# Cross-attention and routed feed-forward: three quarters of the second layer in parts, its relus left in PSUM, and a low part in three pieces

## The reference, cut to what matters

```python
assign = jnp.argmax(x @ centroids.T, axis=1)          # one expert for each token
xn  = layernorm(x) * ln_g[e] + ln_b[e]
h   = relu(einsum('etd,efd->etf', xn, w1) + b1)        # 256 -> 1024
y   = x + einsum('etf,edf->etd', h, w2) + b2           # 1024 -> 256
out = a * y + (1 - a) * x,   a = sigmoid(x @ centroids.T)   # of the chosen expert
```

## Time and profile before

| | |
|---|---|
| median of 3 runs | 1052.74 us (1052.73 to 1053.05) |
| profiled execution, its own time | 1052.73 us |
| its span, first to last instruction | 1050.9 us |
| busy: PE / DVE / ACT / POOL | 1041.6 / 844.9 / 688.7 / 565.3 us |
| granted TensorE clock, mean | 0.999 of full speed |

### The profile page before, as it was taken

One profiled execution on the slowest core, in us unless ns is written; L12 is line 12 of the kernel. 1 busy time (PEld: TensorE's weight loads), 2 busy tenths in 40 slices (PEclk: granted clock), 3 DMA queues, 4 the chain that ended last, 5 costly groups with the idle time before them and its releaser, 6 DMA issues.

```text
span 1050.9 us, 24670 instructions
## 1 busy us (share of the span) xinstructions
PE 1041.6 (99%) x8610; PEld 940.5 (89%) x8610; DVE 844.9 (80%) x1979; ACT 688.7 (66%) x1838; POOL 565.3 (54%) x665
## 2 busy tenths in 40 slices
PE   9999999999999999999999999999999999999997
PEld 7889898988888888889898989889888999999997
DVE  7878888878888888888888879888887797767663
ACT  6765757675666767666757575766566666676761
POOL 1744464646454555545464646465444667566663
PEclk9999999999999999999999999999999999999999
DMA  6665657585757576767667585856356868777760
GB/s 212 160 169 148 170 156 189 146 215 142 201 146 197 142 193 155 200 156 197 159 168 185 142 210 137 213 144 171 91 153 196 307 198 294 250 234 234 249 194 31
DMA packets 159666, 190.57 MB, mean 181 GB/s; under 512 B 17454, under 2 KB 149038, under 8 KB 154673
## 3 DMA queue, kind: packets, MB, share of 16 engines
q1 hardware_dynamic: 155088, 179.09, 62.4%
q0 software_dynamic: 3360, 8.53, 2.2%
q10 hardware_dynamic: 1088, 1.31, 0.4%
HBM read 65.72 MB, written 46.07 MB: 106 GB/s over the span
## 4 chain that ended last, share of the span: by engine, by line
PE 96%; DVE 2%; POOL 1%; ACT 1%; DMA 0%; issue 0%; POOLq 0%; DVEq 0%
PE psum L742 17%; PE psum L775 16%; PE psum L812 11%; PE psum L902 10%; PE psum L791 10%; PE psum L827 9%; PE psum L761 8%; PE psum L938 6%; PE psum L932 5%; PE psum L830 1%; PE psum L883 1%; PE psum L914 1%; DVE neg_max L1410 1%; DMA c_in<-in_ctx_in 0%; PE psum L856 0%; DVE w_lo L1545 0%
## 5 line engine op out<-in xcount | busy, mean ns | idle before, releaser
L1823 POOL TENSOR_TENSOR prob<-prob,inv_sum 128x512 f32<-128x512 f32 x172 | 177.7, 1047 | 190.1 <-DVE inv_sum L1416 189.2
L1133 ACT ACTIVATE prob<-psum,neg_max 128x256 f32<-128x256 f32 x344 | 160.2, 478 | 38.8 <-DVE neg_max L1410 38.5
L1410 DVE TENSOR_REDUCE neg_max<-psum 128x2 f32<-128x512 f32 x256 | 161.9, 672 | 27.7 <-PE psum L791 27.5
L1422 DVE STREAM_TRANSPOSE prob<-prob 128x512 f32<-128x512 f32 x172 | 118.5, 698 | 12.3 <-POOL prob L1823 11.9
L1823 POOL TENSOR_TENSOR w_ring<-w_ring,inv_sum 128x512 f32<-128x512 f32 x76 | 78.1, 1041 | 76.0 <-DVE inv_sum L1416 75.7
L1140 ACT ACTIVATE head_out_hi<-psum 128x512 fp32r<-128x512 f32 x52 | 31.1, 597 | 105.6 <-PE psum L812 102.4
L1119 ACT ACTIVATE v_n<-psum 128x512 f32<-128x512 f32 x128 | 77.9, 608 | 26.7 <-PE psum L775 22.7
L1108 ACT ACTIVATE k_hi<-psum 128x512 fp32r<-128x512 f32 x128 | 77.0, 603 | 22.0 <-PE psum L742 21.3
L1461 DVE TENSOR_TENSOR k_lo<-psum,k_hi 128x512 fp32r<-128x512 f32 x128 | 85.7, 674 | 0.0
L742 PE MATMUL psum<-kv_t_hi,w_hi 128*128 128x512 f32 x252 | 85.0, 419 | 0.0
L775 PE MATMUL psum<-w_hi,kv_t_hi 128*128 128x512 f32 x256 | 80.2, 395 | 0.4 <-DVE k_lo L1461 0.4
(11 more groups left out here) (215 smaller groups left out, 2952.4 us busy)
## 6 DMA issues: line engine op xcount, KB each, us to landing
sorted_rows<-filler SPq DMA_DIRECT2D x54, 660.0 KB
prob_t<-prob SPq DMA_DIRECT2D x172, 128.0 KB, 2.8
w_ring<-prob SPq DMA_DIRECT2D x172, 128.0 KB, 2.7
w<-in_experts SPq DMA_DIRECT2D x19, 1024.0 KB, 7.8
w_ring<-in_experts SPq DMA_DIRECT2D x18, 1024.0 KB, 6.7
prob_t<-w_ring SPq DMA_DIRECT2D x76, 128.0 KB, 2.8
w_ring<-w_ring SPq DMA_DIRECT2D x76, 128.0 KB, 2.7
w_ring<-normed SPq DMA_DIRECT2D x56, 128.0 KB, 3.0
```

What stands on the lines that cost most here:

```text
L1133: act.activation(prob_at(u, bb)[:, :, parity, i], scores_i, ACT.Exp, bias=neg_max[:, at, i:i + 1], accum_out=prob_sum[:, at, i:i + 1]).the ...
L1410: dve.tensor_reduce(neg_max[:, (4 * u + n) % 8, :], psum[:, n, :].rearrange("p (i j) -> p i j", i=2), AXIS_X, ALU.max, negate=True).then_i ...
L1422: dve.transpose(probs, probs).then_inc(s_quad, 1)
L1823: pool.tensor_tensor(probs, probs, inverse, ALU.mult).then_inc(s_soft, 1)
```

## The change

FS goes from 4 to 6: six of the eight chunks of the second layer are in parts, two are plain. The relus of the chunks in parts are written back to the PSUM bank in which they lie, and VectorE splits from there. The bank is then free for the next slot's `layer_1` when VectorE has split it (`f_hl`), not when ScalarE has read it (`f_ha`). ScalarE no longer waits for `hid_raw` to be free, since there is none. GpSimd's low part of w2, now 1536 columns, is made in three instructions of 512; ScalarE's high part is one instruction of 1536. The buffers hid_hi and hid_lo grow and the spacer between them shrinks.

```diff
-            FS = FC // 2
+            FS = 3 * FC // 4
-                sbuf(late, "hid_between", [P, 3 * FS * BLOCK])
+                sbuf(late, "hid_between", [P, (2 * FC + FC // 2 - 2 * FS) * BLOCK])
-            hid_raw = y_t[:].rearrange("p c b t -> p c (b t)")
-            hid_plain = prob_t_even[:].rearrange("p b a h i s q -> p b (a h i s q)").rearrange("p s (f t) -> p s f t", f=FC - FS)
+            hid_plain = prob_t_even[:].rearrange("p b a h i s q -> p (b a h i s q)")[:, FC * BLOCK - 2 * (FC - FS) * BLOCK:].rearrange(
+                "p (s f t) -> p s f t", s=2, f=FC - FS)
 def layer_1(s):
                         if s == 1:
                             pe.wait_ge(s_exp, 8 * n_steps)
+                        elif i < FS // 2:
+                            pe.wait_ge(f_hl, FS // 2 * (s - 1 - FIRST_SPLIT) + i + 1)
                         else:
                             pe.wait_ge(f_ha, FC // 2 * (s - 2) + i + 1)
 def relu_parts(s):
                     if s == FIRST_SPLIT:
-                        wait_low(act, n_pairs - 1, 1)
                         wait_made(act, ("pv", n_steps - 1))
                     for i in range(FC // 2):
                         act.wait_ge(f_h, FC // 2 * (s - 1) + i + 1)
-                        if i < FS // 2 and s > FIRST_SPLIT:
-                            act.wait_ge(f_hl, FS // 2 * (s - 1 - FIRST_SPLIT) + i + 1)
-                        elif i == FS // 2 and s >= 2:
+                        if i == FS // 2 and s >= 2:
                             wait_made(act, ("fy", s - 2, 1))
-                            dst = hid_raw[:, i, at] if f < FS else hid_plain[:, s % 2, f - FS, :]
+                            dst = psum[:, i, at] if f < FS else hid_plain[:, s % 2, f - FS, :]
 def split_hidden(s):
-                        then_next(dve.tensor_copy(hi, hid_raw[:, i, :]))
-                        dve.tensor_tensor(lo, hid_raw[:, i, :], hi, ALU.subtract).then_inc(f_hl, 1)
+                        raw = psum[:, i, :]
+                        then_next(dve.tensor_copy(hi, raw))
+                        dve.tensor_tensor(lo, raw, hi, ALU.subtract).then_inc(f_hl, 1)
 def low_weights_2(s):
-                    pool.tensor_tensor(w2_hl[s % 2][1], raw, w2_hl[s % 2][0], ALU.subtract).then_inc(f_w2l, 1)
+                    hi, lo = w2_hl[s % 2]
+                    for f in range(0, FS, 2):
+                        last = pool.tensor_tensor(lo[:, f:f + 2], raw[:, f:f + 2], hi[:, f:f + 2], ALU.subtract)
+                    last.then_inc(f_w2l, 1)
```

## The result

| | before | after |
|---|---|---|
| median | 1053.05 us (1052.73 to 1054.95, 5 runs) | 1059.09 us (1058.34 to 1060.24, 5 runs) |
| profiled execution, its span | 1052.73, 1050.9 | 1058.34, 1056.5 |
| granted TensorE clock, mean | 0.999 | 0.996 |

The gain on TensorE is there; what it waits for costs twice as much. The busy line of the page after (us, share of the span, instructions), beside the earlier trace rows: TensorE's busy time fell by only 1.4 us, where 5.25 were taken out. That is the first sign that something in it grew.

A forecast was written before the change was run, and what follows sets the result against it. TensorE, busy 99% of the span, was taken as the bound, with VectorE nearly so around slots 1 to 5. 1052.7 - 5.25 (TensorE's work) + 4.2 (waits) = 1051.7 us; range 1049.5 to 1053.5, widened to 1049.0 and 1054.2 towards rivals.

The forecast's parts named there:

- TensorE, -5.25: TensorE's matmuls, 18 slots: two more chunks in parts save 0.29 us a slot, 5.25 us in all; slot 11.80 for 12.09.
- VectorE, the copy from PSUM at 0.67: VectorE's split of hidden banks: copying 512 columns from PSUM takes 0.67 us, so a bank takes 1.34 us.
- What that does to slots 1 to 5, +4.2: Early slots: VectorE's 6.7 us more work makes slot 5's input ready at 872.8; TensorE loses 4.2 us, earlier waits included.
- It does not come on top of the 4.2: Slot 1's late low part: TensorE would wait up to 1.7 us, but VectorE is then ahead by the same stretch.
- GpSimd in three pieces: GpSimd's low part of w2: three pieces of 512 columns take 3.1 to 3.6 us; VectorE's holds total taken as unchanged.
- holds VectorE for at most one piece at a time: GpSimd's low part: VectorE is held for at most one piece of some 1.2 us at a time, but over a longer stretch.
- the sum of the holds as unchanged: VectorE's holds under GpSimd's low parts: some 6 us before, 2.4 less to 1.2 more after; taken as unchanged.
- What costs nothing: ScalarE's longer high part, relus into PSUM (0 to 0.1 us), banks freed by VectorE, dropped waits, late slots' 1.5 us on VectorE.
- The rival on the other side: Late slots: VectorE becomes the bound, held for two pieces, slot 12.3 us, 6 us over 12 slots: 1057.7 us; chance 0.16.

The follow-up runs named there:

- the early low part: Changed kernel, but GpSimd makes the low part of slot 1's w2 before the row scales of the last batch: 1060.49 us, ratio 1.0071.
- the gap: Changed kernel, but GpSimd waits for its own piece of w2's low part to end before issuing the next: 1057.60 us, ratio 1.0043.
- one piece: Changed kernel with GpSimd's low part of w2 in one instruction of 1536 columns instead of three of 512: 1063.05 us, ratio 1.0097.
- the fill: Changed kernel with unused matmuls on TensorE ahead of its waits, four in slot 1's layer 2, eight at slot 5's layer_1: 1058.49 us, ratio 1.0046.
- the kernel from slot 5 on with GpSimd's wait: Changed kernel with four chunks in slots 1 to 4; GpSimd adds the base of slots 4 to 15 after VectorE's input split: 1058.59 us, ratio 1.0039.
- The input first: Changed kernel, but for slots 3 to 5 VectorE splits the next input after the first hidden bank, not the third: 1057.25 us, ratio 1.0039.

## Why the prediction was wrong, point by point

- *TensorE, -5.25:* right; 11.80 us a slot, layer_1 to layer_1.
- *VectorE, the copy from PSUM at 0.67:* right. All 54 casts of line 1644 take 676 to 693 ns and all 54 subtractions of line 1645 take 691 to 694, so none of them was ever held, where before line 1645 took 0.834 in the mean of the late slots. A bank's pitch is 1.32 us against 1.34.
- *What that does to slots 1 to 5, +4.2:* the place was right, and VectorE is what layer_1 waits for, but the input of slot 5 was ready at 876.69 and not at 872.8.
- *"It does not come on top of the 4.2":* this is the step that failed. TensorE's wait for slot 1's low part came (1.77 us; "up to 1.7" was its price), and VectorE's lead was to pay for it. VectorE could not keep the lead, since it needs that layer 2 itself: it stood idle for 0.59 + 2.07 = 2.66 us where the prediction had it without idle time. That is most of the 3.9 us by which slot 5's input was late; a start 0.5 us later, 0.4 us more of holds and 0.3 of the rest make up the others. This is read from the trace; the low part of slot 1 made early took that wait away, and the kernel was no faster, since a cast was then held for 4.60 us.
- *GpSimd in three pieces, "holds VectorE for at most one piece at a time", "the sum of the holds as unchanged":* the sum was right (7.5 us against 7.1 before), the first half was wrong. The cast of line 1628 was held for 3.40 us, through three pieces; with a wait of GpSimd between them no such cast or subtraction lasts over 1.80. That hold fell on the very instruction that TensorE was about to need: with the cast and the subtraction at 0.45 + 0.69 us the input would have been ready at 873.7, 0.4 us behind TensorE's asking at 873.32, and not 3.4. But shorter holds, tried by themselves, did not make the kernel measurably faster, since there were more of them and VectorE was late all the same (0.17 + 2.96 us of waits at layer_1). The Trainium skill, "SBUF — State Buffer", section "Who interferes with whom", says that a VectorE copy in a 2-port mode and GpSimd block each other for the whole instruction. The trace agrees that a copy within SBUF is held (0.42 us by itself, 3.40 here), but by that rule alone the hold would have ended with the piece that it met, at some 873.3 us.
- *The price of a wait:* a term that was missing. Waits of 1.77 and 3.46 us were each followed by matmuls at the lower clock, 1.7 us more apiece. The 1.73 behind slot 5 come on top of all the rest; those of slot 1 are part of why VectorE stood idle.
- *What costs nothing:* the last slot wasn't looked at (0.49 + 0.24 us); and GpSimd's pause near 905 us, 4.62 us long in the trace of before, was in view and not weighed. In the profiled execution of the change it happens to cost nothing, and nothing in two of the others with six chunks there (the early low part, the gap); in seven TensorE waited 1.4 to 4.7 us behind it, and in the last two (one piece, the fill) a wait of 2.77 and of 0.65 us stands a slot later, which wasn't followed up. It lasts 3.87 to 8.00 us, and not longer the later GpSimd comes to it: 3.87 from 906.95 on in the change, 7.74 from 902.65 on in the kernel from slot 5 on with GpSimd's wait. Why is open: the profile names no releaser.

In the prediction's own sum: TensorE's last matmul ends 6.3 us later than -5.25 and +4.2 have it. Slot 5's layer_1 begins 3.9 us late (876.79 for 872.85), the lower clock behind it takes 1.7 and the last slot 0.7. This is one profiled execution taken apart; how the 6 us between the medians divide among these steps no experiment shows.

The rival on the other side had the sign right and the mechanism wrong: it put the loss into the late slots, which ran without a wait, and for the first stretch it named none. The loss is in front of slot 6, 9.2 us of waits and slow clock, and no single repair there made the kernel as fast as before. The input first, the low part early and the wait of GpSimd from slot 5 on each removed or shrank the wait that they aimed at and met another; the gap shortened the holds and left VectorE late.

## What to carry to other kernels

Put extra work only where the engine that gets it has idle time in every slot: with six chunks from slot 10 on (and GpSimd's wait in slots 4 to 7) the kernel is a little faster (0.9987), with six everywhere it is slower (1.0054). Don't set one engine's lead against another's wait before asking whether the first needs what the second makes. Price a wait of TensorE on this kind of chain at its length and, when it is long, at what the lower clock takes behind it (here mostly 1.5 to 1.7 us, at most 2.9). And when two engines hold each other, the sum of the holds isn't enough; ask which instruction will stand under the hold.

## What the hardware did that was not expected

- GpSimd instructions back to back held a VectorE cast for 3.40 us (three pieces of 512 columns), a subtraction for 4.67 and a cast for 4.60 (a base instruction and three pieces), where with a wait between the pieces the longest such hold was 1.80 us. But this isn't so each time. In the changed kernel itself, with no gap added, w_lo (835.57, 3.29 us) and line 1663 (845.01, 1.17 us) got in after one piece, and so did two short instructions of 8 columns in slot 3, under the three pieces from 857.88 to 861.72:
```profile
859.66 0.83 DVE L1603 TENSOR_TENSOR small<-small,taken 128x8 f32<-128x8 f32 x1
860.53 1.22 DVE L1604 SCALAR_TENSOR_TENSOR small<-small,taken 128x8 f32<-128x8 f32 x1
```
  Why these and not the others isn't settled.
- The gap costs 0.4 us a low part (4.20 us against 3.80 for three pieces).
- The clock behind a wait of TensorE, over all the traces here: behind each of the twelve waits of 2.5 to 4.7 us it was at the lower level for a part of the next 6 us, and these matmuls took 1.45 to 2.9 us longer. Of seven waits of 1.77 to 2.35 us three were followed by the lower clock (1.77, 1.81, 1.98) and four were not (1.79, 1.94, 2.02, 2.35). Behind those of 0.38 and 0.49 us in the change it stayed at 1.00, and they cost 0.13 and 0.24 us more than their length.
